# A graph kernel's message stage in groups of 1024 edges instead of 640, with bfloat16 parts summed in PSUM

## The chip, the cores and the metric

The kernel runs on one core of one Trainium2 chip. The metric is device time in microseconds (us), and lower is better. A core has five engines with instruction queues of their own: TensorE (PE; its weight loads are listed as PEld), VectorE (DVE), ScalarE (ACT), GpSimd (POOL) and SyncE (SP). They wait for one another by semaphores. SBUF is the on-chip memory of 128 partitions, PSUM the accumulators that TensorE writes.

## What is computed

A graph of 12,500 nodes with 128 features has 400,000 edges, sorted by target node. Two graph layers run one after the other, each with a residual and a layer norm. The first layer sums neighbours twice; the change leaves it alone. The second layer makes one message for each edge and sums the messages by target:

```python
ef  = relu(edge_attr @ We1 + be1) @ We2 + be2        # 64 -> 128 -> 128, by edge
ef  = ef * sigmoid(ts @ Wt + bt)                     # ts: edge_weight
msg = relu(concatenate([x[row], ef], axis=1) @ Wn1 + bn1) @ Wn2 + bn2
out = segment_sum(msg, col, num_segments=12500) + x
x   = layernorm(x + out)
```

Targets are drawn as 12500 times the square of a uniform number, so that the first nodes have many edges each and the last ones few.

## The kernel before

The program has three stages. Two of them sum neighbours (`sum_neighbours`, tiles named `sum_x_` and `sum_z_`), and the third makes and sums the messages (`sum_messages`, tiles named `messages_`). A tile is 128 edges, one to a partition; there are 3125. The second stage has already written, for each node, `y_d` = its features times the upper half of Wn1, plus the bias, and `rest_d`, what is left of the output beside the message sum.

The third stage goes by groups of 5 tiles (640 edges), 625 in all. In slot `s` of a fully unrolled program every engine has its share of several groups at different lags:

- GpSimd gathers the rows of `y_d` for the source nodes, one indirect DMA a tile (L1630), into a ring of 10 groups (`DEPTH`). It starts group g once the window sums of group g-10 are done (`sums_ready`).
- TensorE (in this order in a slot): `p_hid` of group s from the edge attributes (L1673, float32), `p_msg` of group s-3 (L1679), `p_edge` of group s-1 (L1686), and the window sums of group s-5 (L1696): the message rows times a one-hot matrix of 64 columns, in float32. A float32 product stands in the trace as two matmuls.
- ScalarE: relu to `hid` (L1711), sigmoid to `gate` (L1715), relu of the message rows in place (L1719).
- VectorE: adds a 64-node window to the node sums (L1750), adds `p_msg` to the gathered rows (L1755), makes `gated` = (`p_edge` + bias) times `gate` (L1760), and builds the one-hot matrix (L970).
- SyncE loads attributes and edge weights by bodies of 5 groups, the weights copied to all 128 partitions (L1641, L1644).

Whenever 256 nodes have their sums complete, a piece (`third_nodes`, 49 of them) multiplies them with Wn2, adds `rest_d`, takes the layer norm and stores. The order is written out by hand, by the lags `MSG_LAG, WIN_LAG, ADD_LAG = 3, 5, 6`.

## Time and profile before

| what | us |
|---|---|
| time, median of 3 runs | 9389.36 |
| the 3 runs | 9377.11 to 9419.71 |
| the profiled execution, span from first to last instruction | 9374.2 |
| of it the third stage, from its first gather (4711.19) to the end | 4663 |

The profiled execution's own time is its span; it lies 15 us below the median of the runs. PE is busy for 71% of the span, POOL for 61%, DVE for 46% and ACT for 23%. Busy time of POOL is the making of gathers; issuing a DMA is not counted. "idle <-X" after a row is the time in which the engine did nothing before that instruction, and who released it; "issue" means that the profile shows no wait, and "remote" that it shows a semaphore update with no instruction of this core just before it.

### The profile page before, as it was taken

The page shows a single profiled execution, that of the slowest core. Times are in us where ns is not written, and L with a number is a line of the kernel's source. Part 1 is how long each engine was busy: PE and PEld are TensorE (multiplying, and loading weights), DVE is VectorE, ACT ScalarE, POOL GpSimd, SP SyncE. Part 2 cuts the span into 40 slices and gives each one's busy share as a digit, 9 for nine tenths or more (in the row PEclk, how much of TensorE's full clock was granted, in tenths as well). Part 3 has the DMA queues.
Part 4 walks back from the last instruction along what each step waited for, and adds up shares of the span by engine and source line. Part 5 has one row for each costly group of instructions (what it writes and reads, how often), then busy time and mean ns, then how long its engine had stood idle before and what let it go on. Part 6 is the DMA issues. An engine that isn't in the chain of part 4 may idle for free.

```text
span 9374.2 us, 116910 instructions
## 1 busy us (share of the span) xinstructions
PE 6689.7 (71%) x36831; PEld 4954.1 (53%) x36831; DVE 4268.2 (46%) x9331; ACT 2188.8 (23%) x3195; POOL 5712.6 (61%) x5857
## 2 busy tenths in 40 slices
PE   4667777777656777767657777777777777777777
PEld 3455454444434555555545565565555555555555
DVE  6878777766634444444223233333333333333333
ACT  2111111111110000000023333333333333333333
POOL 6666555555546655655556666666666666666665
PEclk8788888888868888888767777777777777878777
DMA  3456666666647777777533333333333333333333
GB/s 101 128 174 204 200 225 227 221 223 217 223 136 254 243 252 250 257 245 252 192 121 118 109 112 117 109 117 113 110 118 114 110 112 123 112 114 121 113 118 93
DMA packets 585993, 1522.62 MB, mean 162 GB/s; under 512 B 148847, under 2 KB 362243, under 8 KB 558244
## 3 DMA queue, kind: packets, MB, share of 16 engines
q1 hardware_dynamic: 398177, 1131.24, 34.9%
q0 software_dynamic: 187200, 383.76, 14.7%
q8 instruction: 314, 5.14, 0.2%
q14 instruction: 302, 2.47, 0.1%
HBM read 1373.03 MB, written 141.47 MB: 162 GB/s over the span
## 4 chain that ended last, share of the span: by engine, by line
another core or an unknown queue 20%; PE 16%; issue 7%; DVE 4%; ACT 2%; DVEq 1%; DMA 0%; SPq 0%; ACTq 0%
PE messages_p_msg L1679 5%; PE messages_p_edge L1686 5%; PE messages_win L1696 4%; PE messages_p_hid L1673 3%; DVE messages_rows L1755 2%; ACT messages_hid L1711 1%; DVE messages_gated L1760 1%; ACT messages_gate L1715 1%; DVE messages_hot L970 1%; DVEq L62 0%; DVEq L1747 0%; DVE messages_sums L1750 0%; PE messages_win L1538 0%; ACT messages_rows L1719 0%
## 5 line engine op out<-in xcount | busy, mean ns | idle before, releaser
L1630 POOL DMA_INDIRECT messages_rows<-y_d,src_idx x3125 | 2992.2, 957 | 1694.2 <-issue 875.3
L1104 POOL DMA_INDIRECT sum_x_rows<-in_x,sum_x_edges x1525 | 1556.4, 1021 | 1084.4 <-PE sum_x_win L1194 514.6
L1104 POOL DMA_INDIRECT sum_z_rows<-z_d,sum_z_edges x1200 | 1162.6, 969 | 846.0 <-issue 322.4
L1679 PE MATMUL messages_p_msg<-Wm_e,messages_gated 128*128 128x128 f32 x6250 | 1127.9, 343 | 706.4 <-DVE messages_rows L1755 365.8
L1679 PEld LDWEIGHTS messages_p_msg<-Wm_e,messages_gated 128*128 128x128 f32 x6250 | 989.6, 244 | 1037.0 <-issue 996.4
L1755 DVE TENSOR_TENSOR messages_rows<-messages_p_msg,messages_rows 128x640 f32<-128x640 f32 x625 | 513.4, 821 | 1697.2 <-remote 1151.0
L1686 PE MATMUL messages_p_edge<-messages_hid,We 128*128 128x320 f32 x2500 | 1014.7, 539 | 254.7 <-DVE messages_gated L1760 128.3
L1206 PE MATMUL sum_x_build<-sum_x_key_hot,sum_x_low_hot 128*128 128x490 bf16 (+2 forms) x2900 | 869.6, 387 | 338.0 <-DVE sum_x_counts L1402 247.0
L1696 PEld LDWEIGHTS messages_win<-messages_hot,messages_rows 128*128 128x128 f32 x6250 | 947.0, 220 | 237.2 <-issue 164.9
L1696 PE MATMUL messages_win<-messages_hot,messages_rows 128*128 128x64 f32 x6250 | 909.1, 296 | 93.5 <-issue 67.5
L1711 ACT ACTIVATE messages_hid<-messages_p_hid,be 128x640 f32<-128x640 f32 x625 | 495.2, 792 | 1954.4 <-remote 1574.5
L1226 PE MATMUL sum_z_p_loaded<-sum_z_split,sum_z_counts 128*128 128x384 bf16 x2744 | 832.7, 364 | 141.7 <-DMA sum_z_split<-z_parts_d 110.9
L1402 DVE SCALAR_TENSOR_TENSOR sum_x_counts<-sum_x_counts,sum_x_build 128x980 f32 (+3 forms) x635 | 647.7, 1020 | 454.9 <-PE sum_x_build L1206 327.3
L1760 DVE SCALAR_TENSOR_TENSOR messages_gated<-messages_p_edge,be,messages_gate 128x640 f32<-128x640 f32 x625 | 550.6, 881 | 662.8 <-remote 434.1
L1226 PE MATMUL sum_x_p_prod<-sum_x_split,sum_x_counts 128*128 128x385 bf16 x2744 | 705.4, 351 | 180.8 <-DMA sum_x_split<-x_parts_d 144.5
L1686 PEld LDWEIGHTS messages_p_edge<-messages_hid,We 128*128 128x128 f32 x2500 | 543.1, 241 | 443.4 <-issue 317.7
L1190 PEld LDWEIGHTS sum_x_win<-sum_x_hot,sum_x_rows 128*128 128x128 f32 x3050 | 628.6, 223 | 228.7 <-issue 93.1
L1719 ACT ACTIVATE messages_rows<-messages_rows 128x640 f32<-128x640 f32 x625 | 457.8, 733 | 1103.7 <-DVE messages_rows L1755 636.2
L1673 PE MATMUL messages_p_hid<-messages_attr,We 64*128 64x320 f32 x2500 | 581.9, 545 | 185.6 <-ACT messages_hid L1711 157.1
L1402 DVE SCALAR_TENSOR_TENSOR sum_z_counts<-sum_z_counts,sum_z_build 128x784 f32 x325 | 336.6, 1036 | 804.9 <-DMA bm<-in_L_gnn_bn 409.9
L1297 ACT CAST sum_x_hot<-sum_x_hot 128x320 bf16<-128x320 f32 x305 | 139.7, 458 | 2111.8 <-DVE sum_x_hot L970 1436.9
L1190 PE MATMUL sum_x_win<-sum_x_hot,sum_x_rows 128*128 128x64 f32 x3050 | 569.7, 277 | 81.6 <-ACT sum_x_hot L1297 50.6
(250 smaller groups left out, 7916.5 us busy)
## 6 DMA issues: line engine op xcount, KB each, us to landing
sum_x_split<-x_parts_d SPq DMA_DIRECT2D x392, 675.5 KB
sum_z_split<-z_parts_d SPq DMA_DIRECT2D x392, 675.5 KB
messages_when<-in_edge_weight SPq DMA_DIRECT2D x125, 1600.0 KB
messages_attr<-in_edge_attr SPq DMA_DIRECT2D x125, 800.0 KB
counts_d<-sum_x_counts SPq DMA_DIRECT2D x28, 3136.0 KB
sum_z_counts<-counts_d SPq DMA_DIRECT2D x56, 1568.0 KB
messages_rows<-y_d,src_idx POOLq DMA_INDIRECT x3125
sum_x_rows<-in_x,sum_x_edges POOLq DMA_INDIRECT x1525
```

Of the source, the lines that this page charges most:

```text
L1104: nc.gpsimd.indirect_dma_start(out=rows[:, s % depth, j, :], out_offset=None, in_=table, in_offset=bass.IndirectOffsetOnAxis(ap=edges[:, b ...
L1190: last = nc.tensor.matmul(win[g % 2][:, 0:WIN], rows[:, g % depth, j, :], hot[:, q, j, :], start=j == 0, stop=j == TILES - 1)
L1206: last = nc.tensor.matmul(build[i % builds][:, h, 0:columns], low_hot[:, u % lows, :], hot_rooms(u)[:, h * columns:(h + 1) * columns], sta ...
L1226: last = nc.tensor.matmul(product_of(b)[0][:, 0:columns], by_count(b)[:, hi, :], split[:, n % XCHUNKS, hi % CHUNK, 0:columns], start=hi == ...
L1402: nc.vector.scalar_tensor_tensor(nodes, nodes, CARRY_MAX, summed_counts, ALU.min, ALU.add).then_inc(copied, 1)
L1630: nc.gpsimd.indirect_dma_start(out=rows[:, g % DEPTH, j, :], out_offset=None, in_=d["y"], in_offset=bass.IndirectOffsetOnAxis(ap=t.src_idx ...
L1673: last = nc.tensor.matmul(p_hid[:, h, 0:HALF], t.We1[own, :], attr[own, body % LOADS, g % UNROLL, :], start=True, stop=True)
L1679: last = nc.tensor.matmul(msg[:, j * P:(j + 1) * P], gated[:, g % GATEDS, j * P:(j + 1) * P], t.Wm_e[:], start=True, stop=True)
L1686: last = nc.tensor.matmul(p_edge[:, h, 0:HALF], t.We2[:], hid[:, g % HIDS, h, :], start=True, stop=True)
L1696: last = nc.tensor.matmul(win[g % 2][:, 0:WIN], rows[:, g % DEPTH, j, :], hot[:, g % WINDOW_HOTS, j, :], start=j == 0, stop=j == TILES - 1)
L1755: nc.vector.tensor_tensor(at, msg[:, 0:GROUP], at, ALU.add).then_inc(msg_added, 1)
L1760: nc.vector.scalar_tensor_tensor(gated[:, g % GATEDS, :].rearrange("p (h c) -> p h c", h=2), p_edge[:, :, 0:HALF], t.be2[:, 0:1], gate[:, ...
```

## The change

The third stage goes by groups of 8 tiles (1024 edges), 391 of them, and sums nodes in another way.

- The 3125 gathers stay as they are. The ring is 7 groups of 8 tiles, and a group is started when the last part of the group 7 before it has been made (`low_ready`), and no longer when its window sums are done.
- The relu'd message rows are split into three bfloat16 parts that add up to them: ScalarE writes the high part, VectorE subtracts it from the relu (`rest`), ScalarE rounds the rest to the middle part, VectorE subtracts once more for the low part. That is one instruction more on ScalarE and two more on VectorE in each group, for one fewer window addition on VectorE.
- The one-hot matrix has 128 columns in bfloat16. It is now the weights, and the three parts together (384 columns) stream through it. The sums stay in PSUM over a block, a run of tiles whose nodes should span at most 113: 114 blocks in all, the first of 297 tiles, the last ones of 14. At a block's end ScalarE copies the three sums (384 columns), TensorE turns them by three products with the identity (`flip_block`), and VectorE adds them to the node sums.
- The lags are 2 for `p_msg` and 5 for the window sums. These stand second in TensorE's slot. A block's turn stands first in the next slot, and a piece's product now stands ahead of `p_edge`.
- `hid` has 2 buffers for 3, `gate` 3 for 4, `gated` 2 for 3. SyncE loads by groups of 8 tiles, 3 groups ahead.
- Once, in slots 8 to 13, VectorE does some 60 small instructions that find out whether the plan fits the data, on top of the conversion of the target numbers that it did before.

TensorE in the middle of the stage, one slot before:

```order
L1673 MATMUL messages_p_hid<-messages_attr,We 128x320 x2
L1679 MATMUL messages_p_msg<-Wm_e,messages_gated 128x128 x5
L1686 MATMUL messages_p_edge<-messages_hid,We 128x320 x2
L1696 MATMUL messages_win<-messages_hot,messages_rows 128x64 x5
L1673 MATMUL messages_p_hid<-messages_attr,We 128x320 x2
```

and after, two slots, in the first of which a block has ended:

```order
L1738 MATMUL messages_win<-identity,messages_product 128x128 x3
L1771 MATMUL messages_p_hid<-messages_attr,We 128x512 x2
L1756 MATMUL messages_win<-messages_parts,messages_hot 128x384 x8
L1779 MATMUL messages_p_msg<-Wm_e,messages_gated 128x128 x8
L1791 MATMUL messages_p_edge<-messages_hid,We 128x512 x2
L1771 MATMUL messages_p_hid<-messages_attr,We 128x512 x2
L1756 MATMUL messages_win<-messages_parts,messages_hot 128x384 x8
L1779 MATMUL messages_p_msg<-Wm_e,messages_gated 128x128 x8
L1791 MATMUL messages_p_edge<-messages_hid,We 128x512 x2
L1738 MATMUL messages_win<-identity,messages_product 128x128 x3
```

The window sums went from the end of the slot to its start, the turn of a block stands ahead of everything, and a group has 4 + 8 + 16 + 4 = 32 matmuls of the trace for 8 tiles where it had 4 + 10 + 4 + 10 = 28 for 5.

VectorE in the middle of the stage, one slot before (names: `messages_hot` is the one-hot matrix, `messages_rows` the gathered rows):

```order
L970 TENSOR_TENSOR messages_hot<-iota,rel 128x320
L1747 TENSOR_LOAD base_int
L1747 ISA x2
L1750 ISA
L1750 TENSOR_TENSOR messages_sums<-messages_sums,messages_win 128x64
L1755 TENSOR_TENSOR messages_rows<-messages_p_msg,messages_rows 128x640
L1760 SCALAR_TENSOR_TENSOR messages_gated<-messages_p_edge,be,messages_gate 128x640
```

and after, a slot that begins with a block's addition (`messages_parts` are the bfloat16 parts):

```order
L1864 TENSOR_LOAD messages_bases
L1864 ISA x2
L1867 ISA
L1867 TENSOR_TENSOR messages_sums<-messages_sums,messages_win 128x128
L1884 TENSOR_TENSOR messages_parts<-messages_rows,messages_parts 128x8x128
L1887 SCALAR_TENSOR_TENSOR messages_rows<-messages_rows,messages_parts 128x1024
L1893 TENSOR_TENSOR messages_rows<-messages_p_msg,messages_rows 128x1024
L1898 SCALAR_TENSOR_TENSOR messages_gated<-messages_p_edge,be,messages_gate 128x1024
L1903 TENSOR_TENSOR messages_hot<-iota,rel 128x1024
L1884 TENSOR_TENSOR messages_parts<-messages_rows,messages_parts 128x8x128
```

Three instructions now read two tiles of SBUF each (`parts`, `rows`, `hot`), and they stand one behind another around the end of a slot; before there was one, the one-hot, of 320 elements.

The core of the diff:

```diff
+SPAN, BLOCK_NODES = 8, 113
+SPAN_DEPTH, SPAN_PARTS, SPAN_HOTS = 7, 3, 3
+SPAN_LOADS, SPAN_AHEAD = 4, 3
+SPAN_HIDS, SPAN_GATES, SPAN_GATEDS = 2, 3, 2
+SPAN_MSG_LAG, SPAN_WIN_LAG = 2, 5
+SPAN_SPACING, SPAN_SOON, SPAN_CHECK = 3, 16, 12
...
-                wait_for(pool, sums_ready, g - DEPTH + 1)
+            for g in range(plan.groups):
+                if g in (0, SPAN_SOON):
+                    pool.wait_ge(keep_in[1 if g else 0], 48)
+                wait_for(pool, low_ready, g - SPAN_DEPTH + 1)
                 pool.sem_inc(gathers_started, 1)
-                for j in range(TILES):
+                for j in range(tiles_of(g)):
+                    at = g * SPAN + j
                     nc.gpsimd.indirect_dma_start(
-                        out=rows[:, g % DEPTH, j, :], out_offset=None, in_=d["y"],
-                        in_offset=bass.IndirectOffsetOnAxis(ap=t.src_idx[:, g, j:j + 1], axis=0)).then_inc(rows_arrived[g % DEPTH], 16)
-            for q in range(DEPTH):
-                pool.wait_ge(rows_arrived[q], len(range(q, m.NG, DEPTH)) * 16 * TILES)
+                        out=rows[:, g % SPAN_DEPTH, j, :], out_offset=None, in_=d["y"],
+                        in_offset=bass.IndirectOffsetOnAxis(ap=src_idx[:, at:at + 1], axis=0)).then_inc(rows_arrived[g % SPAN_DEPTH], 16)
...
+            def load_group(g):
+                own = g % SPAN_LOADS
+                wait_for(sp, hid_summed, g - SPAN_LOADS + 1)
+                sp.dma_start(attr[:, own], d["span_attr"][g]).then_inc(attr_arrived[own], 16)
+                wait_for(sp, gate_ready, g - SPAN_LOADS + 1)
+                sp.dma_start(when[:, own], d["edge_weight"][g * SPAN * P:(g + 1) * SPAN * P].partition_broadcast(P)
                              ).then_inc(when_arrived[own], 16)
...
+            def flip_block(b):
+                pe.wait_ge(block_copied, b + 1)
+                for i in range(SPLITS):
+                    last = nc.tensor.matmul(win[b % 2][:, 0:P], product[:, b % 2, i * P:(i + 1) * P], t.identity[:],
+                                            start=i == 0, stop=i == SPLITS - 1)
+                last.then_inc(block_flipped, 1)
+
+            def open_block(b, s):
+                wait_for(pe, block_added, b - 1)
...
+            def window_sums(g, s):
+                pe.wait_ge(low_ready, g + 1)
+                pe.wait_ge(hot_ready, g + 1)
+                for j in range(tiles_of(g)):
+                    b = plan.block_of[g * SPAN + j]
+                    begin, end = plan.blocks[b]
+                    if g * SPAN + j == begin:
+                        open_block(b, s)
+                    last = nc.tensor.matmul(win[b % 2][:, 0:SPLITS * P], hot[:, g % SPAN_HOTS, j, :], parts[:, g % SPAN_PARTS, j, :],
+                                            start=g * SPAN + j == begin, stop=g * SPAN + j == end - 1)
+                last.then_inc(win_summed, 1)
...
+                for b in ended_at[s - 1] if s else []:
+                    flip_block(b)
...
+                for g in groups(s, SPAN_WIN_LAG):
+                    window_sums(g, s)
+                for g in groups(s, SPAN_MSG_LAG):
                     pe.wait_ge(gated_ready, g + 1)
                     wait_for(pe, msg_added, g)
-                    for j in range(TILES):
-                        last = nc.tensor.matmul(msg[:, j * P:(j + 1) * P], gated[:, g % GATEDS, j * P:(j + 1) * P], t.Wm_e[:],
+                    for j in range(tiles_of(g)):
+                        last = nc.tensor.matmul(p_msg[:, j * P:(j + 1) * P], gated[:, g % SPAN_GATEDS, j * P:(j + 1) * P], t.Wm_e[:],
                                                 start=True, stop=True)
                     last.then_inc(msg_summed, 1)
...
+                for g in groups(s, SPAN_MSG_LAG + 1):
+                    act.wait_ge(rest_ready, g + 1)
+                    nc.scalar.copy(part(g, 1), room(g)).then_inc(middle_ready, 1)
...
-                    nc.scalar.activation(rows[:, g % DEPTH], rows[:, g % DEPTH], ACT.Relu).then_inc(msg_ready, 1)
+                    wait_for(act, win_summed, g - SPAN_PARTS + 1)
+                    nc.scalar.activation(part(g, 0), room(g), ACT.Relu).then_inc(high_ready, 1)
...
+                for b in ended_at[s]:
+                    act.wait_ge(win_summed, s - SPAN_WIN_LAG + 1)
+                    wait_for(act, block_flipped, b - 1)
+                    nc.scalar.copy(product[:, b % 2], win[b % 2][:, 0:SPLITS * P]).then_inc(block_copied, 1)
...
+                nc.vector.tensor_copy(tile_bases[:, own], tile_bases[:, own].bitcast(I32)).then_inc(rel_ready, 1)
+                dve.wait_ge(rel_ready, 4 * i + 2)
+                nc.vector.tensor_tensor(rel[:, own], rel[:, own], tile_bases[:, own], ALU.subtract).then_inc(rel_ready, 1)
+                dve.wait_ge(rel_ready, 4 * i + 3)
+                nc.vector.memset(tile_bases[:, own], 0.0).then_inc(rel_ready, 1)
...
+            def add_block(b):
+                nodes = ds(dve.value_load(bases[0:1, b:b + 1], min_val=0, max_val=m.N), P)
+                dve.wait_ge(block_flipped, b + 1)
+                wait_for(dve, block_added, b)
+                nc.vector.tensor_tensor(sums[:, nodes], sums[:, nodes], win[b % 2][:, 0:P], ALU.add).then_inc(block_added, 1)
...
+                for g in groups(s, SPAN_MSG_LAG + 2):
+                    dve.wait_ge(middle_ready, g + 1)
+                    nc.vector.tensor_tensor(part(g, 2), room(g), part(g, 1), ALU.subtract).then_inc(low_ready, 1)
+                for g in groups(s, SPAN_MSG_LAG + 1):
+                    dve.wait_ge(high_ready, g + 1)
+                    nc.vector.scalar_tensor_tensor(room(g), room(g), 0.0, part(g, 0), ALU.max, ALU.subtract).then_inc(rest_ready, 1)
+                for g in groups(s, SPAN_MSG_LAG):
+                    before = sum(16 * tiles_of(i) for i in range(g % SPAN_DEPTH, g + 1, SPAN_DEPTH))
+                    dve.wait_ge(rows_arrived[g % SPAN_DEPTH], before)
                     dve.wait_ge(msg_summed, g + 1)
-                    at = rows[:, g % DEPTH].rearrange("p j f -> p (j f)")
-                    nc.vector.tensor_tensor(at, msg[:, 0:GROUP], at, ALU.add).then_inc(msg_added, 1)
+                    at = room(g).rearrange("p j f -> p (j f)")
+                    nc.vector.tensor_tensor(at, p_msg[:, edges_of(g)], at, ALU.add).then_inc(msg_added, 1)
                 for g in groups(s, 1):
                     dve.wait_ge(gate_ready, g + 1)
                     dve.wait_ge(edge_summed, g + 1)
-                    wait_for(dve, msg_summed, g - GATEDS + 1)
-                    nc.vector.scalar_tensor_tensor(gated[:, g % GATEDS, :].rearrange("p (h c) -> p h c", h=2),
-                                                   p_edge[:, :, 0:HALF], t.be2[:, 0:1],
-                                                   gate[:, g % GATES], ALU.add, ALU.mult).then_inc(gated_ready, 1)
-                for g in groups(s, MSG_LAG):
-                    wait_for(dve, sums_ready, g - WINDOW_HOTS + 1)
-                    one_hot(nc, t, hot[:, g % WINDOW_HOTS], t.rel[:, g, :]).then_inc(hot_ready, 1)
+                    wait_for(dve, msg_summed, g - SPAN_GATEDS + 1)
+                    nc.vector.scalar_tensor_tensor(gated[:, g % SPAN_GATEDS, :], p_edge[:], t.be2[:, 0:1],
+                                                   gate[:, g % SPAN_GATES], ALU.add, ALU.mult).then_inc(gated_ready, 1)
+                for g in groups(s, SPAN_WIN_LAG - 1):
+                    n = tiles_of(g)
+                    wait_for(dve, win_summed, g - SPAN_HOTS + 1)
+                    nc.vector.tensor_tensor(
+                        hot[:, g % SPAN_HOTS, 0:n], t.iota[:].unsqueeze(1).to_broadcast([P, n, P]),
+                        rel[:, g * SPAN:g * SPAN + n].unsqueeze(2).to_broadcast([P, n, P]), ALU.is_equal).then_inc(hot_ready, 1)
```

## Rows read from the trace of the kernel before

**Rows 1.** The page: span, then busy time of each engine.
```profile
span 9374.2 us, 116910 instructions
...
PE 6689.7 (71%) x36831; PEld 4954.1 (53%) x36831; DVE 4268.2 (46%) x9331; ACT 2188.8 (23%) x3195; POOL 5712.6 (61%) x5857
```

**Rows 2.** Windows: us; busy (instructions) PE, PEld, DVE, ACT, POOL; PEclk; DMA; GB/s.
```profile
6000.00:7000.00 1000.00, 742.97 (x3834) 582.80 (x3834) 317.74 (x607) 337.52 (x439) 645.51 (x676) 0.78 0.36 113
```

**Rows 3.** Groups by line, 4711-9374 us: busy us, mean ns, idle before, releasers.
```profile
L1630 POOL DMA_INDIRECT messages_rows<-y_d,src_idx x3125 | 2992.2, 957 | 1694.2 <-issue 875.3 <-remote 490.9 <-PE messages_win L1696 268.1
L1679 PE MATMUL messages_p_msg<-Wm_e,messages_gated 128*128 128x128 f32 x6250 | 1127.9, 343 | 706.4 <-DVE messages_rows L1755 365.8 <-issue 340.0
L1686 PE MATMUL messages_p_edge<-messages_hid,We 128*128 128x320 f32 x2500 | 1014.7, 539 | 254.7 <-DVE messages_gated L1760 128.3 <-issue 74.1 <-ACT messages_hid L1711 51.9
...
L1696 PE MATMUL messages_win<-messages_hot,messages_rows 128*128 128x64 f32 x6250 | 909.1, 296 | 93.5 <-issue 67.5 <-DVE messages_piece_u L1546 25.2
L1673 PE MATMUL messages_p_hid<-messages_attr,We 64*128 64x320 f32 x2500 | 581.9, 545 | 185.6 <-ACT messages_hid L1711 157.1 <-issue 14.5 <-DMA messages_attr<-in_edge_attr 13.3
...
L1755 DVE TENSOR_TENSOR messages_rows<-messages_p_msg,messages_rows 128x640 f32<-128x640 f32 x625 | 513.4, 821 | 1697.2 <-remote 1151.0 <-PE messages_p_msg L1679 315.6 <-issue 230.3
...
L970 DVE TENSOR_TENSOR messages_hot<-iota,rel 128x320 f32<-128x320 f32 x625 | 303.6, 486 | 0.0
```

**Rows 4.** Timeline, a steady stretch: start us, us, engine, line, idle before.
```profile
6503.57 0.94 POOL L1630 DMA_INDIRECT messages_rows<-y_d,src_idx  x1 [2.76 <-PE messages_win L1696]
...
6504.53 2.50 PE L1679 MATMUL messages_p_msg<-Wm_e,messages_gated 128*128 128x128 f32 x10
...
6507.14 0.82 DVE L1755 TENSOR_TENSOR messages_rows<-messages_p_msg,messages_rows 128x640 f32<-128x640 f32 x1 [1.91 <-PE messages_p_msg L1679]
...
6510.34 1.38 PE L1679 MATMUL messages_p_msg<-Wm_e,messages_gated 128*128 128x128 f32 x10
...
6517.11 0.82 DVE L1755 TENSOR_TENSOR messages_rows<-messages_p_msg,messages_rows 128x640 f32<-128x640 f32 x1 [7.00 <-remote]
...
6525.61 0.94 POOL L1630 DMA_INDIRECT messages_rows<-y_d,src_idx  x1 [3.44 <-remote]
```

**Rows 5.** Timeline, same stretch: one-hot instruction and two gathers.
```profile
6504.62 0.48 DVE L970 TENSOR_TENSOR messages_hot<-iota,rel 128x320 f32<-128x320 f32 x1
...
6504.81 1.11 POOL L1630 DMA_INDIRECT messages_rows<-y_d,src_idx  x1 [0.30 <-issue]
...
6506.23 0.94 POOL L1630 DMA_INDIRECT messages_rows<-y_d,src_idx  x1 [0.30 <-issue]
```

**Rows 6.** Timeline, first stage: VectorE instructions and gathers under them.
```profile
128.01 1.08 DVE L1406 TENSOR_TENSOR sum_x_counts<-sum_x_counts,sum_x_split 128x896 f32<-128x896 f32 x1
128.04 1.87 POOL L1104 DMA_INDIRECT sum_x_rows<-in_x,sum_x_edges  x1 [0.30 <-issue]
...
1000.92 0.82 DVE L1382 TENSOR_TENSOR sum_x_low_hot<-iota,sum_x_low_part 128x640 bf16<-128x640 f32 x1
1001.28 1.35 POOL L1104 DMA_INDIRECT sum_x_rows<-in_x,sum_x_edges  x1 [1.78 <-remote]
...
1002.42 1.17 DVE L1402 SCALAR_TENSOR_TENSOR sum_x_counts<-sum_x_counts,sum_x_build 128x980 f32 x1
1002.93 0.94 POOL L1104 DMA_INDIRECT sum_x_rows<-in_x,sum_x_edges  x1 [0.30 <-issue]
```

**Rows 7.** Timeline: POOL near the start and end of the stage.
```profile
4711.19 0.94 POOL L1630 DMA_INDIRECT messages_rows<-y_d,src_idx  x1 [59.55 <-DMA rel<-in_dst_tiles]
...
4786.30 0.95 POOL L1630 DMA_INDIRECT messages_rows<-y_d,src_idx  x1 [12.77 <-PE messages_win L1696]
...
9337.04 0.95 POOL L1630 DMA_INDIRECT messages_rows<-y_d,src_idx  x1 [0.30 <-issue]
```

**Rows 8.** Groups by line, 0-4700 us: forms like the added ones.
```profile
L1226 PE MATMUL sum_z_p_loaded<-sum_z_split,sum_z_counts 128*128 128x384 bf16 x2744 | 832.7, 364 | 141.7 <-DMA sum_z_split<-z_parts_d 110.9 <-issue 19.4 <-DVE sum_z_sums L1331 5.7
...
L1235 PE MATMUL sum_z_p_loaded<-identity,sum_z_loaded_product 128*128 128x128 f32 x168 | 37.3, 380 | 24.1 <-ACT sum_z_loaded_product L1314 21.1 <-issue 3.1
```

## Prediction before the run

> **What bounds the kernel now.** I read the page first, for the whole span [rows 1]; then the windows of the third stage [rows 2] and its groups by line [rows 3], for who is busy and who waits; then a steady stretch of the timeline [rows 4], to see which wait ends last.
>
> The third stage's gathers run from 4711.19 to 9337.99 us [rows 7], 4626.8 us for 3125 gathers, 1.48 us each. POOL's busy time is 2992.2 us (957 ns each) and its idle time 1694.2 us, of which 59.55 us stand before the first gather [rows 3, 7]. About 0.30 us between two gathers is issue [rows 5], in all 3124 x 0.30 = 937 us. So a gather that nobody disturbs costs 0.945 + 0.30 = 1.25 us, and 1694.2 - 59.55 - 937 = 697 us are real waits. Without waits or disturbance the gathers would need 3125 x 1.25 = 3906 us: the floor of this stage. It is a floor that the change can't lower, since it keeps all gathers.
>
> Why does POOL wait? TensorE's four groups of matmuls are busy 1127.9 + 1014.7 + 909.1 + 581.9 = 3633.6 us [rows 3], which is 5.81 us in each of the 625 slots, while a slot lasts 4626.8 / 625 = 7.40 us. The 1.6 us between is what TensorE loses by waiting (and by the pieces). The timeline shows one way in which it is lost [rows 4]. TensorE's `p_msg` ends at 6504.53 + 2.50 = 6507.03, and the row addition of VectorE starts 0.11 us later. The next `p_msg` ends at 6510.34 + 1.38 = 6511.72, but VectorE, which has been idle for 7.00 us, starts its addition only at 6517.11, 5.4 us late. Between the two POOL had begun a train of gathers, and the late one is released by "remote". I read this so: after some microseconds of unbroken gathers, TensorE's completions reach the others late. The row addition's idle time is 1697.2 us in the stage, 1151.0 us of it "remote" [rows 3]. So the loop is TensorE, late signal, VectorE, TensorE; once the ring is full, POOL waits for the loop too, mostly 2.8 to 3.4 us at a time [rows 4]. Neither engine alone is the bound: POOL's floor is 3906 us, TensorE's busy time 3634 us.
>
> **The change: TensorE.** Hidden layer, edge and message products keep their work for a tile: (581.9 + 1014.7 + 1127.9) / 3125 = 0.872 us. The window sum of a tile goes from 909.1 / 3125 = 0.291 us to one bfloat16 product of 384 columns. The second stage has that shape: 832.7 / 2744 = 0.303 us [rows 8]. New are 114 turns of 3 products, each two matmuls in the trace: 684 x 37.3 / 168 = 152 us, 0.049 us for a tile [rows 8]. Sum 1.224 us, 9.79 us for a group of 8. Together 3825 us, 190 us more than now; it is hidden where TensorE waits anyway, and its price is bounded by 0 and 190 us. What the change saves is slots: 391 for 625, so 234 times fewer crossings from TensorE to another engine and back. If a slot goes on losing 1.6 us, TensorE's loop lasts 9.79 + 1.63 = 11.42 us, 391 of them 4465 us, against 4627 us now. The granted clock is 0.78 in the middle of the stage [rows 2], and I leave it there: fewer matmuls stand for a tile (4.0 instead of 5.6), but they are longer.
>
> **VectorE.** Three instructions now have two inputs in SBUF and 1024 elements: `low`, `rest` and the one-hot. The nearest rows are 0.82 us for 640 and 1.08 us for 896 elements [rows 6], which continued gives about 1.21 us for 1024. The row addition becomes 0.821 + 384 x 0.001 = 1.2 us, `gated` about the same. That is some 6.2 us in a slot of 11.4 us, so VectorE is no bound by itself; DVE is busy 318 us in 1000 now [rows 2].
>
> Their effect on GpSimd is a cost, though. A gather that begins under such an instruction ends only after it. The one-hot of 0.48 us makes a gather 1.11 us, the next gather has 0.94 us [rows 5]. The one of 0.82 us makes it 1.35 us, that of 1.08 us makes it 1.87 us; and a VectorE instruction of 1.17 us that reads one of its inputs from PSUM leaves it at 0.94 us [rows 6]. If instructions fall at random in a train with a gather each 1.25 us, one of length d holds a gather with probability d / 1.25, for d / 2 on average: d x d / 2.5. For 0.486 us this gives 0.094 us; the trace has 3125 x (957 - 945) ns = 37.5 us over 625 one-hots, 0.06 us each [rows 3], 64% of it. For 1.21 us the formula gives 0.586 us, 64% of it is 0.375 us. The group has three of them close together, which makes it likelier that a gather meets one, so I take 0.45 us, between the two. There are 3 x 391 = 1173: **528 us**. The ends are 0.1 us each (117 us, if gathers slip between them as they mostly do with the one-hot now) and 0.586 us each (687 us). The one-hots' present 37 us are in the 528, since I count from the undisturbed gather.
>
> The Trainium skill has a rule for this ("SBUF — State Buffer", section "Who interferes with whom"): a VectorE instruction with two SBUF inputs contends with a GpSimd instruction that reads SBUF, and whoever comes second blocks. By that rule, the trace agrees that the gather is held (1.87 for 0.94 us) and that one PSUM input avoids it. It speaks against this change, which moves work from TensorE's window product to exactly such instructions. In full it would make each of the 1173 hold POOL for its whole 1.21 us; that is the fourth case below.
>
> **ScalarE.** 338 us busy in 1000 now [rows 2], for three instructions of 640 elements in a slot. One more, and 1024 for 640 elements: (338 x 4 / 3) per edge, 45% busy. Hidden, at no cost unless the loop below takes it in. **SyncE** issues two loads a group, 782 where it had 250. TensorE waits 13.3 us in the stage for them now [rows 3]; cover is 3 groups, some 34 us. Nothing.
>
> **The ring.** 7 x 8 = 56 tiles for 50, and a place is free at `low`, 4 slots after the slot number of its group, where it was 5 slots. In time that is 4 x 11.6 = 46 us for 5 x 7.4 = 37 us. The first ring of gathers is followed now by a wait of 12.77 us [rows 7], which stays about as it is.
>
> **Ends.** After the last gather come 36 us now (9374.2 - 9337.99). The last slots are longer and hold one step more: +20 us (bounds 0 and 40). The 60 small checks of VectorE in slots 8 to 13 lie under the full ring of gathers.
>
> **Sum.** Gathers 3906 + holds 528 = 4434 us; TensorE's loop is at 4465 us, so the two meet, and I add 100 us of waits (bounds 0 and the present 697): 4534 us. Against 4627 us that is -93. With the end +20: -73. The profiled execution, 9374.2 us, becomes 9301 us; the median of the runs lies 15 us above it: **9315 us**.
>
> **Rivals.**
> *B, TensorE's late completions keep the loop long (slower).* With POOL's trains unbroken, lateness may grow with the train instead of counting by slot. The row addition then waits in VectorE's queue with `gated` and the one-hot behind it, and TensorE waits for both. If a slot loses twice what it loses now, 3.26 us, it lasts 13.05 us, 391 of them 5103 us: +476, with the end +20 and the 15: 9885 us. It decides from the point where TensorE's idle time in a slot is over 1.8 us (then the loop passes 4534). For it: 1151.0 us of "remote" [rows 3]. Against it: an unbroken train is what makes them late, and B itself breaks the trains.
> *C, the holds stay small and the waits go.* 3906 + 117 + 100 = 4123 us: -504, so 9374.2 - 504 + 20 + 15 = 8905 us. For it: TensorE at full pace would do it, and the trace has 0.06 us a hold now. Against it: TensorE's loop would have to lose little in a slot, 4123 / 391 - 9.79 = 0.75 us.
> *D, each two-input instruction holds POOL in full.* 1173 x 1.21 = 1419 us: 3906 + 1419 + 100 = 5425 us, +798, 10,207 us. The trace speaks against it, since a hold ends with the instruction (1.35 us for 0.82).
> *E, the plan doesn't fit the data.* Then the stage is made a second time in the general way, 14,000 us or more. Blocks are cut at 113 expected nodes for 128 columns, so I give it next to nothing.
>
> **Chances.** The forecast 0.38; its own range is 9180 to 9440 us, since a hold of 0.375 or 0.586 us instead of 0.45 moves it by -88 or +159 us, and waits of 50 instead of 100 us by -50; B (9440 to 9990) 0.30; C (8800 to 9180) 0.27; D and E 0.05. The range leaves out the fast third of C and a tail of B with D: 8880 to 9870. A measurement of this kernel can tell about 0.5% from no change, 9342 to 9436 us. Faster: C and two thirds of the forecast's case, 0.52. Within: 0.11. Slower: the rest, 0.37.
>
> **What would show it.** The mean of one gather in the profile after: 945 + 1173 x 0.45 / 3125, about 1.11 us, in my case; 0.98 in C; 1.4 in D. POOL's idle time in the stage beyond the first and 0.30 us a gather: about 100 us in my case, 600 in B. The granted clock near 0.78; `win` near 0.30 us a product; `low`, `rest` and the one-hot near 1.2 us. I am wrong if these instructions are much shorter or longer, if the window product costs over 0.4 us, or if something that no row shows (bfloat16 writes, ScalarE's four instructions) becomes the end of the chain.

## The result, and the profile after

The changed kernel takes 9569.73 us (median of 4 runs, 9541.55 to 9598.91), the kernel before beside it 9386.33 us. The ratio is **1.0191**, with a 95% interval of 1.017 to 1.0212: 1.9% slower. I had forecast 9315 us and 0.8% faster. The time lies outside my own range (9180 to 9440 us) and in that of my rival B (9440 to 9990 us), 3% under its price of 9885 us.

Span and busy time of each engine, from the page of the changed kernel (before: [rows 1]):

```profile
span 9539.4 us, 104096 instructions
...
PE 6088.1 (64%) x32520; PEld 3959.4 (42%) x32520; DVE 5222.8 (55%) x8964; ACT 2481.2 (26%) x2996; POOL 6116.3 (64%) x5857
```

TensorE has 600 us less to do than before, VectorE 950 us more, and the whole is 165 us longer. The groups by line of the third stage, changed kernel; they answer to [rows 3] (busy us, mean ns | idle before, releasers):

```profile
L1699 POOL DMA_INDIRECT messages_rows<-y_d,src_idx x3125 | 3388.0, 1084 | 1436.0 <-issue 950.8 <-DVE messages_parts L1884 424.4 <-DMA messages_sums<-in_message_base 60.8
...
L1779 PE MATMUL messages_p_msg<-Wm_e,messages_gated 128*128 128x128 f32 x6250 | 875.0, 300 | 49.0 <-DVE messages_gated L1898 49.0
L1791 PE MATMUL messages_p_edge<-messages_hid,We 128*128 128x512 f32 x1564 | 740.9, 595 | 6.3 <-issue 6.3
L1756 PE MATMUL messages_win<-messages_parts,messages_hot 128*128 128x384 bf16 x3125 | 731.4, 388 | 1450.6 <-DVE messages_hot L1903 1150.9 <-issue 296.7 <-DVE messages_piece_u L1552 2.8
...
L1893 DVE TENSOR_TENSOR messages_rows<-messages_p_msg,messages_rows 128x1024 f32<-128x1024 f32 x391 | 478.4, 1224 | 1930.3 <-remote 1223.1 <-PE messages_p_msg L1779 349.2 <-DMA messages_rows<-y_d,src_idx 213.6
...
L1771 PE MATMUL messages_p_hid<-messages_attr,We 64*128 64x512 f32 x1564 | 479.5, 692 | 48.0 <-issue 18.4 <-ACT messages_hid L1802 16.2 <-DMA messages_attr<-in_span_attr 13.3
...
L1884 DVE TENSOR_TENSOR messages_parts<-messages_rows,messages_parts 128x1024 bf16<-128x1024 f32 x391 | 475.9, 1217 | 0.0
...
L1738 PE MATMUL messages_win<-identity,messages_product 128*128 128x128 f32 x684 | 126.2, 330 | 465.7 <-ACT messages_product L1822 323.3 <-issue 142.5
```

The last gather, which answers to [rows 7]:

```profile
9472.43 0.95 POOL L1699 DMA_INDIRECT messages_rows<-y_d,src_idx  x1 [0.31 <-issue]
```

From these rows the books of GpSimd can be made as in the prediction. From the first to the last gather it is 9473.4 - 4710.2 = 4763 us (4627 before). The undisturbed gathers are 3906 us as ever. What the gathers take above 0.945 us is 3388.0 - 2953 = 435 us (39 before; I forecast 528). The rest, 4763 - 3906 - 435 = 422 us, are waits (682 before by the same sum; I forecast 100). So +396 of holds and -260 of waits make +136 us, and the tail behind the last gather grew from 36 to 66 us (I forecast 56). The prediction had 697 us for the waits before, because it took 0.30 us between two gathers; the median gap is 0.305 us in both traces, and only with that do the 3906 us come out.

Those books tell where GpSimd's time went, not why it waited 422 us. TensorE's five groups are busy 875.0 + 740.9 + 731.4 + 479.5 + 126.2 = 2953 us, 7.6 us of a slot of 4763 / 391 = 12.2 us. It loses 4.6 us a slot, where it lost 1.6. Not all of that is a loss that a better order could win back. The gathers of a slot with their holds take (3906 + 435) / 391 = 11.1 us, and TensorE can't be faster than that: 3.5 of the 4.6 us are GpSimd's pace, and in 1.1 us GpSimd waits too. Before the change the two were 0.5 and 1.1 us.

Two rows name the waits: 1450.6 us before the window sums, 1150.9 of them for the one-hot (before the change all idle time before them was 93.5 us), and 1930.3 us of VectorE before the row addition, 1223.1 of them "remote".

The timeline has two states. This is the good one, from the middle of the stage (start us, us, engine, line, idle before):

```profile
6306.33 1.97 POOL L1699 DMA_INDIRECT messages_rows<-y_d,src_idx  x1 [0.30 <-issue]
...
6308.44 1.88 PE L1791 MATMUL messages_p_edge<-messages_hid,We 128*128 128x512 f32 x4
...
6308.71 1.23 DVE L1893 TENSOR_TENSOR messages_rows<-messages_p_msg,messages_rows 128x1024 f32<-128x1024 f32 x1 [1.23 <-PE messages_p_msg L1779]
...
6310.41 1.28 DVE L1898 SCALAR_TENSOR_TENSOR messages_gated<-messages_p_edge,be,messages_gate 128x1024 f32<-128x1024 f32 x1 [0.48 <-PE messages_p_edge L1791]
...
6311.61 1.21 DVE L1903 TENSOR_TENSOR messages_hot<-iota,rel 128x1024 bf16<-128x1024 f32 x1
...
6312.97 1.46 PE L1756 MATMUL messages_win<-messages_parts,messages_hot 128*128 128x384 bf16 x8 [1.59 <-DVE messages_hot L1903]
...
6313.95 1.97 POOL L1699 DMA_INDIRECT messages_rows<-y_d,src_idx  x1 [0.30 <-issue]
...
6314.27 1.95 PE L1779 MATMUL messages_p_msg<-Wm_e,messages_gated 128*128 128x128 f32 x16
...
6316.32 1.23 DVE L1893 TENSOR_TENSOR messages_rows<-messages_p_msg,messages_rows 128x1024 f32<-128x1024 f32 x1 [1.23 <-PE messages_p_msg L1779]
```

A slot lasts 6316.32 - 6308.71 = 7.61 us, for 8 tiles. It is a closed chain: `p_edge` ends at 6310.32, then `gated`, then the one-hot to 6312.82, and only then TensorE's window sums, for which it has been idle 1.59 us, then `p_msg` and `p_edge`. In each slot one gather lasts 1.97 us, begun under `rest`, and one 1.3 us, begun under the one-hot; the others take 0.94 us. GpSimd makes 5 gathers in such a slot where 8 tiles are used up, so the rows run out: counted from the gathers and row additions of the trace, 40 tiles were ready beyond the one in use at 6261 us, and 3 at 6378 us. This state can't last, but it isn't an empty ring that ends it here: no row addition between the two times waits for rows. Then comes the bad state:

```profile
6383.97 1.95 PE L1779 MATMUL messages_p_msg<-Wm_e,messages_gated 128*128 128x128 f32 x16
...
6396.12 1.23 DVE L1893 TENSOR_TENSOR messages_rows<-messages_p_msg,messages_rows 128x1024 f32<-128x1024 f32 x1 [10.99 <-remote]
...
6404.52 1.28 DVE L1898 SCALAR_TENSOR_TENSOR messages_gated<-messages_p_edge,be,messages_gate 128x1024 f32<-128x1024 f32 x1 [7.17 <-remote]
...
6407.08 2.72 PE L1756 MATMUL messages_win<-messages_parts,messages_hot 128*128 128x384 bf16 x8 [18.39 <-DVE messages_hot L1903]
...
6409.59 2.51 PE L1779 MATMUL messages_p_msg<-Wm_e,messages_gated 128*128 128x128 f32 x16
...
6417.62 2.08 PE L1771 MATMUL messages_p_hid<-messages_attr,We 64*128 64x512 f32 x4 [3.80 <-issue]
...
6443.74 0.94 POOL L1699 DMA_INDIRECT messages_rows<-y_d,src_idx  x1 [0.30 <-issue]
6452.19 1.23 DVE L1893 TENSOR_TENSOR messages_rows<-messages_p_msg,messages_rows 128x1024 f32<-128x1024 f32 x1 [42.22 <-remote]
...
6455.88 2.72 PE L1756 MATMUL messages_win<-messages_parts,messages_hot 128*128 128x384 bf16 x8 [36.19 <-DVE messages_hot L1903]
...
6457.68 1.15 POOL L1699 DMA_INDIRECT messages_rows<-y_d,src_idx  x1 [13.00 <-DVE messages_parts L1884]
```

`p_msg` ends at 6385.92 and its row addition starts at 6396.12, 10 us late, though the gathers of its group were made by 6383.39. The next ends at 6412.10, and its addition starts at 6452.19, **40 us late**, with VectorE idle for 42.22 us and TensorE, which needs the one-hot queued behind that addition, for 36.19 us. In these 40 us GpSimd makes gather upon gather of 0.95 us with nothing to hold it, until at 6444.68 its ring is full; it stands still, and 7.5 us later the addition starts, with `gated` ready right behind it. The trace also has records of many semaphore updates themselves. TensorE's update for this addition is recorded at 6452.10, 40 us behind the product, and that of the window sums, whose last product ended at 6409.80, at 6438.03. Over the stage, the recorded updates of VectorE and ScalarE stand 0.01 us behind the instruction's end (the median), and about 1% are over 1 us behind. Of those behind `p_msg`, 34% are over 1 us late (67% in the kernel before). What tips the good state into the bad one is not shown: the episode before this one began with 18 tiles ready, this one with 3. The windows of the two states and of the stage's middle (which answers to [rows 2]):

```profile
6284.00:6352.00 68.00, 54.10 (x280) 32.85 (x279) 48.67 (x43) 37.01 (x35) 54.28 (x46) 0.95 0.46 137
6396.00:6452.00 56.00, 8.82 (x32) 4.79 (x32) 6.53 (x9) 4.24 (x4) 37.10 (x39) 0.56 0.22 60
6000.00:7000.00 1000.00, 553.12 (x2690) 330.46 (x2690) 487.75 (x474) 376.00 (x367) 713.76 (x658) 0.81 0.38 109
```

The granted clock is 0.95 in the good state and 0.56 in the bad one, where TensorE is busy for 8.82 of 56 us: it falls after TensorE has stood idle (18.39 us, then 36.19 us), and it is a consequence here.

### The profile page after: what moved, and what is told of

It is laid out like the page before. It is cut to its first block, busy times and chain, and to the rows that moved or that the text cites. A ratio compares the mean times of both kernels' runs of the same rounds, so it can differ in the third digit from the quotient of the medians.

```text
span 9539.4 us, 104096 instructions
## 1 busy us (share of the span) xinstructions
PE 6088.1 (64%) x32520; PEld 3959.4 (42%) x32520; DVE 5222.8 (55%) x8964; ACT 2481.2 (26%) x2996; POOL 6116.3 (64%) x5857
## 4 chain that ended last, share of the span: by engine, by line
another core or an unknown queue 14%; PE 13%; DVE 10%; issue 6%; POOL 6%; ACT 1%; DVEq 0%; DMA 0%; SPq 0%; POOLq 0%; ACTq 0%
POOL messages_rows L1699 6%; PE messages_p_msg L1779 5%; PE messages_win L1756 4%; PE messages_p_edge L1791 3%; DVE messages_hot L1903 3%; DVE messages_gated L1898 2%; DVE messages_rows L1893 2%; DVE messages_rows L1887 1%; DVE messages_parts L1884 1%; PE messages_p_hid L1771 1%; PE messages_win L1738 1%; DVEq L68 0%; ACT messages_product L1822 0%; DVE messages_sums L1867 0%
## 5 line engine op out<-in xcount | busy, mean ns | idle before, releaser
L1699 POOL DMA_INDIRECT messages_rows<-y_d,src_idx x3125 | 3388.0, 1084 | 1436.0 <-issue 950.8
L1756 PE MATMUL messages_win<-messages_parts,messages_hot 128*128 128x384 bf16 x3125 | 731.4, 388 | 1450.6 <-DVE messages_hot L1903 1150.9
L1893 DVE TENSOR_TENSOR messages_rows<-messages_p_msg,messages_rows 128x1024 f32<-128x1024 f32 x391 | 478.4, 1224 | 1930.3 <-remote 1223.1
L1756 PEld LDWEIGHTS messages_win<-messages_parts,messages_hot 128*128 128x128 bf16 x3125 | 316.8, 110 | 2017.4 <-issue 1897.1
L1779 PE MATMUL messages_p_msg<-Wm_e,messages_gated 128*128 128x128 f32 x6250 | 875.0, 300 | 49.0 <-DVE messages_gated L1898 49.0
L1814 ACT ACTIVATE messages_parts<-messages_rows 128x1024 bf16<-128x1024 f32 x391 | 412.2, 1054 | 1433.2 <-DVE messages_rows L1893 954.6
L1791 PE MATMUL messages_p_edge<-messages_hid,We 128*128 128x512 f32 x1564 | 740.9, 595 | 6.3 <-issue 6.3
L1898 DVE SCALAR_TENSOR_TENSOR messages_gated<-messages_p_edge,be,messages_gate 128x1024 f32<-128x1024 f32 x391 | 501.2, 1282 | 329.1 <-remote 197.8
L1802 ACT ACTIVATE messages_hid<-messages_p_hid,be 128x1024 f32<-128x1024 f32 x391 | 434.3, 1111 | 734.1 <-remote 394.0
L1394 DVE TENSOR_SCALAR sum_x_key_hot<-columns,sum_x_key 128x980 bf16<-128x980 f16 (+3 forms) x1600 | 608.3, 422 | 25.7 <-remote 19.3
L1805 ACT CAST messages_parts<-messages_rows 128x1024 bf16<-128x1024 f32 x391 | 407.9, 1043 | 766.9 <-DVE messages_rows L1887 553.8
```

The lines of the kernel that those rows point to most:

```text
L1394: nc.vector.tensor_scalar(hot_rooms(u), t.columns[:, 0:columns], key[:, ring, at:at + 1], None, ALU.is_equal).then_inc(key_hot_ready, 1)
L1699: nc.gpsimd.indirect_dma_start(out=rows[:, g % SPAN_DEPTH, j, :], out_offset=None, in_=d["y"], in_offset=bass.IndirectOffsetOnAxis(ap=src_ ...
L1756: last = nc.tensor.matmul(win[b % 2][:, 0:SPLITS * P], hot[:, g % SPAN_HOTS, j, :], parts[:, g % SPAN_PARTS, j, :], start=g * SPAN + j == ...
L1779: last = nc.tensor.matmul(p_msg[:, j * P:(j + 1) * P], gated[:, g % SPAN_GATEDS, j * P:(j + 1) * P], t.Wm_e[:], start=True, stop=True)
L1791: last = nc.tensor.matmul(p_edge[:, own], t.We2[:], hid[:, g % SPAN_HIDS, own], start=True, stop=True)
L1893: nc.vector.tensor_tensor(at, p_msg[:, edges_of(g)], at, ALU.add).then_inc(msg_added, 1)
```

## The experiments

Theory L: while GpSimd makes gathers without a break, TensorE's completions reach the others late, the more the longer the train; a break in the train lets them in. (I call a break a pause or a standstill below; GpSimd may be busy in it, but makes no gather.) Theory H is the one of my prediction: two-input instructions of VectorE hold gathers and are a pure cost. Theory C: the change made the loop longer by its order, above all the one-hot behind `gated`. "Slot" is below the mean time between two row additions, from all of them in a trace. All ratios are to the kernel before on the same chip; the chips differ by 1.4% (medians of before from 9384 to 9512 us), so spans are compared by ratio. The slots are not scaled, and no difference of them under 1.4% is read. "Held" is what the gathers take above 0.945 us each; the last column sums the releasers other than issue and the load before the first gather (waits ahead of a pause too), and holds the 0.30 us of issue of each wait.

| kernel | ratio, 95% interval | slot, us | held, us | waits for the ring, us |
|---|---|---|---|---|
| before | 1 | 7.41 (5 tiles) | 39 | 759 |
| changed | 1.0191 (1.017 to 1.0212) | 12.27 | 435 | 424 |
| a_depth4 | 1.0251 (1.0223 to 1.0279) | 12.53 | 426 | 567 |
| a_reduce2 | 1.0699 (1.067 to 1.0728) | 13.58 | 100 | 1277 |
| a_reduce2_pause | 1.0126 (1.0091 to 1.016) | 12.07 | 153 | 0, and 759 of pauses |
| a_hotfirst | 1.0091 (1.0067 to 1.0116) | 12.12 | 579 | 250 |
| a_hotflip | 1.0047 (1.0033 to 1.0061) | 11.89 | 613 | 136 |
| a_hotflip_pause | 1.0253 (1.0222 to 1.0285) | 12.50 | 562 | 2, and 475 of pauses |
| a_hotflip_two | 1.0403 (1.037 to 1.0435) | 12.93 | 166 | 962 |
| b_hold | 1.000 (0.9984 to 1.0017) | 7.51 | 246 | 596 |
| b_pause | 0.997 (0.9955 to 0.9985) | 7.48 | 34 | 517, and 339 of pauses |
| b_pause_mid | 0.9941 (0.9924 to 0.9958) | 7.34 | 39 | 187, and 572 of pauses |
| b_pause_long | 0.9912 (0.9882 to 0.9943) | 7.33 | 15 | 17, and 759 of pauses |
| b_pause_eight | 1.0018 (1.0002 to 1.0033) | 7.43 | 26 | 336, and 474 of pauses |

**The loop without gathers.** The third stage gathers its first ring and goes on with stale rows: `for g in range(plan.groups)` on GpSimd becomes `for g in range(SPAN_DEPTH)` (`DEPTH` in the kernel before), and VectorE waits for the first ring alone.

> The changed kernel, but the third stage gathers only its first ring (56 tiles) and then goes on adding to the stale rows; all other instructions stay. Theory L (late signals: TensorE's completions reach VectorE and ScalarE late while GpSimd gathers without a break, the more the longer the train): every slot is as short as the short ones of the full kernel, 7.6 us, so the stage lasts 391 x 7.6 + 60 = 3030 us and the span is about 7,750 us. Rival S (TensorE's loop is slow by itself, whatever GpSimd does): slots stay at 12.2 us on average, and the span stays within 2% of 9540 us.

> The kernel before, with gathers for the first ring (50 tiles) alone, the rest of the stage on stale rows. Theory L: slots of about 4.4 us, 625 x 4.4 + 60 = 2810 us, span about 7,520 us, so that the loop of before is, for a tile, a little faster than that of the change. Rival S: slots stay at 7.4 us, span about 9,370 us.

Measured: spans of 8060.8 and 7511.3 us, 0.848 and 0.790 of before. TensorE in the kernel before, and in the changed one, from 5000 to 6000 us:

```profile
5000.00:6000.00 1000.00, 1000.00 (x6690) 804.53 (x6689) 546.72 (x1014) 580.64 (x746) 0.00 (x0) 1.00 0.33 119
```

```profile
5000.00:6000.00 1000.00, 796.60 (x4259) 471.16 (x4256) 778.06 (x703) 583.16 (x553) 0.00 (x0) 1.00 0.33 104
```

Rival S is gone: without gathers the slots are 4.31 us before and 8.28 us after the change. Late completions are gone as well: in the kernel before without gathers, under 1% of the recorded updates behind `p_msg` are over 1 us late. But for the changed kernel I had expected 7.6, and this is the first finding on the change itself. Before, TensorE is busy all of the time at full clock. In the changed kernel it is busy 80%: its loop is no longer its own work but the chain through VectorE. For the whole stage the loop alone is 391 x 8.28 = 3237 us against 625 x 4.31 = 2694 us, **543 us more**, although TensorE has less to do. With gathers this is no loss of 543 us, since GpSimd's floor of 3906 us stands above both loops. What it can take away is the room to catch up after a late completion.

**Is it GpSimd, or the traffic?** In one kernel every second tile is gathered after the first ring; in the other SyncE loads all rows, the same number of bytes to the same places, in plain transfers:

```diff
-                for j in range(tiles_of(g)):
+                for j in range(0, tiles_of(g), 1 if g < SPAN_DEPTH else 2):
```

```diff
+            def load_rows(g):
+                wait_for(sp, low_ready, g - SPAN_DEPTH + 1)
+                for j in range(tiles_of(g)):
+                    first = (g * SPAN + j) * 37 % (m.N // P) * P
+                    sp.dma_start(rows[:, g % SPAN_DEPTH, j, :], d["y"][first:first + P]).then_inc(rows_arrived[g % SPAN_DEPTH], 16)
```

> The changed kernel with only every second tile gathered after the first ring (1,594 gathers for 3,125; the other tiles use stale rows). By the runs, the first ring alone gives 8,061 us and all gathers 9,540 us. Theory N (each gather costs TensorE's loop the same, 0.48 us): 8,061 + 1,538 x 0.48 = 8,800 us. Theory L (what costs is unbroken trains; a half-loaded GpSimd waits for its ring most of the time): under 8,450 us.

> The changed kernel with all rows of the third stage loaded by SyncE in plain transfers of 128 x 512 bytes (the rows are then others than the graph's; GpSimd makes one gather for a spare tile and no more): the same bytes into the same places, no indirect transfers. Theory G (what makes TensorE's completions late is GpSimd making gathers): as without gathers, about 8,061 us, delays over 5 us nearly none. Rival D (it is the traffic of the rows on the transfer engines and in SBUF): delays stay, and the span is over 9,200 us.

Measured: 8010 and 7951 us in all, 0.853 and 0.847 of before on their chip, as without any gathers (0.848). The windows of the two:

```profile
5000.00:6000.00 1000.00, 797.11 (x4250) 471.17 (x4248) 775.38 (x707) 583.89 (x556) 522.96 (x517) 1.00 0.45 138
```

```profile
5000.00:6000.00 1000.00, 798.03 (x4258) 472.23 (x4256) 775.74 (x711) 585.66 (x558) 0.00 (x0) 1.00 0.54 171
```

With 171 GB/s moved for 109 in the full kernel nothing is late (no "remote" before the row addition, 1223.1 us in the full kernel), so it is not the traffic. And 517 gathers in 1000 us, in trains of four, cost TensorE nothing: slots of 8.27 us, 57.1 us of "remote". A price of 0.48 us for each gather is refuted. The full kernel's slot is 4 us longer, with 658 gathers in 1000 us in trains of 50 on average, but that compares unlike things: GpSimd alone needs 11.1 us for a slot's gathers there. What is left for the late completions is the making of gathers on GpSimd. That it takes an unbroken train, the pauses below show, with all gathers made.

**The ring.** `SPAN_DEPTH` 7 to 4.

> The changed kernel with a ring of 4 groups (32 tiles) for 7, nothing else. Theory L: GpSimd reaches the end of its ring sooner, so that each late episode is cut short after some 20 gathers: the longest delay of a row addition behind its product falls from 40 us to under 20, trains get shorter, and the time is 9,250 to 9,540 us in spite of the smaller ring. Rival R (the ring is what covers GpSimd's waits): GpSimd's waits grow from 420 us, the time is over 9,650 us.

1.0251 against 1.0191 of the changed kernel. The longest delay of a row addition behind its product fell from 56 to 25 us (I had read 40 and expected under 20), but those over 5 us went from 68 to 94, and GpSimd waits 567 us. The time I expected under L, 9,250 to 9,540 us, was too low (1.0251 of 9386 us is 9622 us): cutting episodes short paid less than the smaller ring cost.

**Without two thirds of the holds.** `rest` and `low` become one-input reductions of the same length (1209 and 1208 ns for 1217 and 1216), and what they should have made is left out:

```diff
-                    nc.vector.tensor_tensor(part(g, 2), room(g), part(g, 1), ALU.subtract).then_inc(low_ready, 1)
+                    nc.vector.tensor_reduce(taken[:, g % 4, 0:tiles_of(g)], room(g), axis=AX.X, op=ALU.max).then_inc(low_ready, 1)
```

> The changed kernel with rest and low (two SBUF inputs each) replaced by reductions of the same 1024 elements with one input; what they should have made is left out, so the middle and low parts are wrong. Only the one-hot still has two SBUF inputs. Theory H (the holds are what the change costs): what gathers take above 0.945 us falls from 435 us to about 145 us, and the time falls by as much, to about 9,280 us. Theory L (the time is set by late signals): the holds fall alike, but GpSimd's unbroken trains make TensorE late as often or more, GpSimd waits more instead, and the time stays within 1% of 9,570 us or rises.

```profile
L1700 POOL DMA_INDIRECT messages_rows<-y_d,src_idx x3125 | 3053.4, 977 | 2296.2 <-DVE messages_taken L1887 1276.6 <-issue 954.1 <-DMA messages_sums<-in_message_base 65.5
...
L1896 DVE TENSOR_TENSOR messages_rows<-messages_p_msg,messages_rows 128x1024 f32<-128x1024 f32 x391 | 478.4, 1224 | 2443.1 <-remote 1922.6 <-PE messages_p_msg L1780 341.6 <-issue 178.9
```

The holds fell as theory H said, from 435 to 3053.4 - 2953 = 100 us. And the kernel became 5% **slower**. "Remote" before the row addition rose from 1223.1 to 1922.6 us, GpSimd's waits from 424.4 to 1276.6 us. Nothing in VectorE's times differs; its instructions just no longer stop GpSimd, as the timeline shows for a gather under a reduction:

```profile
6614.27 1.21 DVE L1890 TENSOR_REDUCE messages_taken<-messages_rows 128x8 f32<-128x1024 f32 x1
6614.35 0.94 POOL L1700 DMA_INDIRECT messages_rows<-y_d,src_idx  x1 [0.31 <-issue]
```

So the holds had kept a part of TensorE's completions on time: a part, since 1223.1 us of "remote" stand in the changed kernel with them.

**A standstill instead of the holds.** The same kernel, and GpSimd clears a tile nobody reads (1320 elements on a partition) after each 5 gathers:

```diff
+                    if at and at % 5 == 0:
+                        wait_for(pool, paused, at // 5 - 1)
+                        nc.gpsimd.memset(still[:], 0.0).then_inc(paused, 1)
```

> The kernel in which rest and low are one-input reductions (their results left out; 1.070 of before), and GpSimd clears a tile of 1320 elements (by the 0.54 us of 512 elements about 1.4 us) after each 5 gathers: 624 pauses as long as a held gather, 870 us in all. Theory P (the relief that two-input instructions give TensorE is that GpSimd stands still for over a microsecond): late row additions get much rarer (sum of delays over 1 us from 1,720 us to under 900) and the time falls to 0.99 to 1.04 of before, in spite of the pauses. Rival Q (the relief has to do with VectorE's second port or with when the holds fall, not with the standstill): delays stay, and the time stays at 1.07 or rises.

```profile
L1704 POOL DMA_INDIRECT messages_rows<-y_d,src_idx x3121 | 3101.9, 994 | 863.9 <-issue 863.9
...
L1703 POOL MEMSET messages_still<- 128x1320 f32 x624 | 759.2, 1217 | 0.2
...
L1900 DVE TENSOR_TENSOR messages_rows<-messages_p_msg,messages_rows 128x1024 f32<-128x1024 f32 x391 | 478.4, 1224 | 2189.4 <-DMA messages_rows<-y_d,src_idx 2056.5 <-PE messages_p_msg L1784 115.4 <-issue 17.5
```

Adding 759 us of work to the engine that was said to be the bound takes 5.4% off: 1.0126, less than the changed kernel. GpSimd waits for nobody, and the row addition's idle time has changed its releaser from "remote" to the arrival of rows. The pauses last 1.22 us, not the 1.4 I assumed. One sign that I had named did not come: the delays over 1 us sum to 1203 us, not under 900. But the additions now wait for rows; none is "remote" any more, and of the recorded updates behind `p_msg` 5% are over 1 us late (60% in a_reduce2). Theory P holds: the relief is the break in the gathers, whoever brings it about.

**The chains of the change.** The one-hot moves from the end of VectorE's slot to its start (a_hotfirst), and in addition the block's turn from ahead of `p_hid` to behind it (a_hotflip), so that `p_hid` may cover ScalarE's copy.

```diff
+                for g in groups(s, SPAN_WIN_LAG - 1):
+                    n = tiles_of(g)
+                    wait_for(dve, win_summed, g - SPAN_HOTS + 1)
...
                 for g in groups(s, SPAN_MSG_LAG + 2):
                     dve.wait_ge(middle_ready, g + 1)
```

```diff
-                for b in ended_at[s - 1] if s else []:
-                    flip_block(b)
...
                     last.then_inc(hid_summed, 1)
+                for b in ended_at[s - 1] if s else []:
+                    flip_block(b)
                 for g in groups(s, SPAN_WIN_LAG):
                     window_sums(g, s)
```

> The changed kernel with one edit: VectorE makes the one-hot of a slot before the other instructions of the slot (ahead of low), not after gated. Theory C (the change has put the one-hot at the end of a closed chain: row addition, gated, one-hot, window sums, p_msg): TensorE no longer waits for it, the 1150.9 us of idle time before the window sums nearly go, and a late row addition no longer stops the window sums; 150 to 350 us less than the changed kernel, about 9,300 us (scaled to the chip of that profile). Theory L alone (only late signals and gathers count): the lost time moves to another wait, and the time stays within 0.7% of the changed kernel.

> The same edit in the kernel that gathers its first ring alone (stale rows after it). Theory C: slots fall from 8.28 us on average to about 7.0 us, the span from 8,061 us to about 7,560 us, since TensorE needs 6.4 us a slot at full clock. If VectorE or ScalarE is the next bound, they stay above 7.6 us and the span above 7,800 us.

> The changed kernel with the one-hot first in VectorE's slot (as in the run before) and a block's turn on TensorE behind p_hid, not ahead of it, so that ScalarE's copy of the block is covered by p_hid. Theory C (closed chains that the change made are a part of the loss): TensorE's wait for the copy (323 us before the turn's products in the changed kernel) goes, and 30 to 100 us of it are gained over the kernel with the one-hot first, which was at 1.009 of before: 0.998 to 1.006 of before. Theory L alone (only gathers and late signals): within 0.3% of 1.009.

> The kernel with the one-hot first and the turn behind p_hid, gathering its first ring alone (stale rows after it). Theory C (these two chains are what the change lengthened): the mean slot falls from 8.28 us in the changed kernel and 7.83 us with the one-hot first to about 7.2 us, the span from 7,914 to about 7,670 us. If the bound is VectorE's own work (some 6.9 us a slot with pieces), no less than 7.4 us and 7,740 us.

```profile
L1699 POOL DMA_INDIRECT messages_rows<-y_d,src_idx x3125 | 3532.2, 1130 | 1257.7 <-issue 947.2 <-DVE messages_parts L1890 250.4 <-DMA messages_sums<-in_message_base 60.0
...
L1756 PE MATMUL messages_win<-messages_parts,messages_hot 128*128 128x384 bf16 x3125 | 669.3, 358 | 239.1 <-issue 158.4 <-DVE messages_piece_u L1552 53.3 <-DVE messages_parts L1890 27.4
...
L1899 DVE TENSOR_TENSOR messages_rows<-messages_p_msg,messages_rows 128x1024 f32<-128x1024 f32 x391 | 477.8, 1222 | 1824.9 <-remote 951.3 <-DMA messages_rows<-y_d,src_idx 689.6 <-PE messages_p_msg L1779 145.7
```

```profile
L1699 POOL DMA_INDIRECT messages_rows<-y_d,src_idx x3125 | 3566.0, 1141 | 1156.1 <-issue 949.7 <-DVE messages_parts L1890 136.4 <-DMA messages_sums<-in_message_base 69.9
...
L1899 DVE TENSOR_TENSOR messages_rows<-messages_p_msg,messages_rows 128x1024 f32<-128x1024 f32 x391 | 478.0, 1223 | 1846.9 <-DMA messages_rows<-y_d,src_idx 1292.4 <-remote 475.3 <-issue 40.4
```

Alone, the loop falls from 8.28 to 7.83 and to 7.23 us a slot (I had expected 7.0 and 7.2 us); 391 x 7.23 = 2827 us still is 133 us more than before the change. With gathers, the time falls from 1.0191 to 1.0091 and to 1.0047 of before: 1.4 of the 1.9% lay in these two places. The gain of the first was below the 150 us that I expected, since the waits moved: the row addition now waits for rows (213.6, then 689.6, then 1292.4 us "<-DMA"), while "remote" falls from 1223.1 to 951.3 and 475.3 us. In a_hotflip GpSimd hardly waits (136.4 us), and gathers hold 613 us. It is the bound there: 3906 + 613 + 134 us of waits are all of its 4652 us from the first gather to the last, 25 us more than before the change. What the waits gave back (682 to 134 us), the holds took (39 to 613 us). One thing did not go as expected: the turn's products wait for ScalarE's copy for 428.2 us in a_hotflip and 398.6 us in a_hotfirst (323.3 in the changed kernel). That wait fell only in the loops without gathers, from 343.7 to 232.0 us. So the turn's new place helps, and not by hiding the copy as I had thought.

**Are the holds a cost now?** Two kernels from a_hotflip: a pause of 1.22 us after each 8 gathers; and two bfloat16 parts instead of three, so that `low`, a third of the two-input instructions, is left out, the sums are a little less exact, and TensorE streams 256 columns for 384. GpSimd is then released by `middle_ready`.

```diff
-                    nc.vector.tensor_tensor(part(g, 2), room(g), part(g, 1), ALU.subtract).then_inc(low_ready, 1)
...
-                    last = nc.tensor.matmul(win[b % 2][:, 0:SPLITS * P], hot[:, g % SPAN_HOTS, j, :], parts[:, g % SPAN_PARTS, j, :],
+                    last = nc.tensor.matmul(win[b % 2][:, 0:2 * P], hot[:, g % SPAN_HOTS, j, :], parts[:, g % SPAN_PARTS, j, 0:2 * P],
```

> The kernel with the one-hot first and the turn behind p_hid (1.005 of before), and GpSimd clears a tile of 1320 elements (about 1.4 us) after each 8 gathers, 390 pauses or 550 us. If late signals are still what costs, delays fall and the time falls to 0.98 to 1.00 of before. If GpSimd itself is the bound by now (it waits 134 us in the stage, and 613 us go into held gathers), the pauses come on top in good part: 1.02 to 1.05.

> The kernel with the one-hot first and the turn behind p_hid, and the message rows split into two bfloat16 parts, not three: low is left out, with 390 of the two-input instructions, and TensorE streams 256 columns for 384. GpSimd is started again when the middle part is made. If GpSimd and its holds are the bound by now: a third of the 613 us of holds goes, 0.975 to 0.99 of before. If the holds are needed as relief, delays grow instead and the time is 1.00 to 1.03.

```profile
L1699 POOL DMA_INDIRECT messages_rows<-y_d,src_idx x3125 | 3119.3, 998 | 1972.2 <-ACT messages_parts L1805 961.8 <-issue 945.4 <-DMA messages_sums<-in_message_base 64.9
...
L1896 DVE TENSOR_TENSOR messages_rows<-messages_p_msg,messages_rows 128x1024 f32<-128x1024 f32 x391 | 478.3, 1223 | 2228.1 <-remote 1986.6 <-PE messages_p_msg L1779 180.7 <-issue 60.4
```

The pauses end the late completions (9.2 us of "remote" before the row addition) and still cost: from the first gather to the last the stage takes 4885 us for 4652, since GpSimd is the bound. But taking holds away is worse still: the held time falls from 613 to 166 us, and the ratio is 1.0403, over the 1.00 to 1.03 that I expected, with 1986.6 us of "remote". Both neighbours of a_hotflip are slower. So the holds are not all waste there either: the `low` instructions take time of GpSimd, and without them the waits grow by more.

**The kernel before.** Two more one-hot matrices in each slot that nobody reads (b_hold), and pauses of 0.54, 1.22 and, by 960 elements, 0.92 us after each 5 gathers, and of 1.22 us after each 8.

```diff
+                    for i in range(2):
+                        nc.vector.tensor_tensor(extra[:, 2 * (g % 4) + i], t.iota[:].unsqueeze(1).to_broadcast([P, TILES, P]),
+                                                t.rel[:, g].unsqueeze(2).to_broadcast([P, TILES, P]), ALU.is_equal)
```

```diff
+                if g:
+                    wait_for(pool, paused, g - 1)
+                    nc.gpsimd.memset(still[:], 0.0).then_inc(paused, 1)
                 wait_for(pool, sums_ready, g - DEPTH + 1)
```

> The kernel before, and VectorE makes two one-hot matrices of 640 elements more in each slot, right after its own, which nobody reads: two more instructions of about 0.8 us with two SBUF inputs, 1,250 in all. Theory H (holds are a pure cost): each holds GpSimd by 0.17 to 0.26 us, so 210 to 330 us more, about 9,640 us on a chip with 9,386 us for the kernel before. Theory L with relief (a held gather gives TensorE's completions time to arrive): row additions that start over 1 us behind their product get rarer (188 before), and the time stays within 1% of before or falls.

> The kernel before, and GpSimd clears a small tile (512 elements on each partition, nobody reads it) once in each group of 5 gathers: a pause in the making of gathers of 0.4 to 1 us. Theory L with relief: TensorE's completions arrive promptly (sum of delays over 1 us from 1,982 us to under 1,000), GpSimd's waits for the ring nearly vanish, since the pauses take their place; time between -1% and +3% of before, by the length of the pause. Rival (it is not the making of gathers but GpSimd being busy at all that delays them): delays stay, waits stay, and the pauses come on top, 250 to 600 us.

> The kernel before with a pause of about 1.4 us (a tile of 1320 elements cleared) after each 5 gathers, where 0.54 us gave 0.997. GpSimd's floor becomes 3906 + 624 x 1.27 = 4,700 us for the stage, 70 us over its present 4,627. Theory P (a standstill over a microsecond is the relief): delays of row additions over 1 us fall from about 2,000 us to under 900, waits for the ring vanish, GpSimd alone is the bound: 1.005 to 1.015. Rival Q: delays stay as they are and the time is over 1.03.

> The kernel before with a pause by a tile of 960 elements, about 0.9 us, after each 5 gathers (0.54 us gave 0.997, 1.22 us gave 0.991 and no wait for the ring any more, so that GpSimd alone was the bound). GpSimd's floor is here some 3906 + 624 x 0.8 = 4,400 us, against 4,590 us used with the long pause. If a standstill of 0.9 us relieves enough: 0.975 to 0.99. If relief sets in only above it: waits for the ring come back to 200 us or more and the time is 0.99 to 1.00.

> The kernel before with the pause of 1.22 us after each 8 gathers, not 5: 390 pauses, GpSimd's floor some 3906 + 390 x 1.08 = 4,330 us. If what counts is the length of each pause: 0.97 to 0.99. If it is the number of gathers between two pauses (TensorE falls behind within a train of 8): waits for the ring come back, 0.99 to 1.01.

```profile
L1631 POOL DMA_INDIRECT messages_rows<-y_d,src_idx x3125 | 3199.6, 1024 | 1546.2 <-issue 888.3 <-remote 458.7 <-PE messages_win L1697 137.2
...
L1756 DVE TENSOR_TENSOR messages_rows<-messages_p_msg,messages_rows 128x640 f32<-128x640 f32 x625 | 513.5, 822 | 1426.1 <-remote 1228.4 <-PE messages_p_msg L1680 128.1 <-issue 68.0
```

```profile
L1634 POOL DMA_INDIRECT messages_rows<-y_d,src_idx x3125 | 2968.1, 950 | 921.5 <-issue 847.8 <-DMA rel<-in_dst_tiles 56.9 <-PE messages_win L1700 10.1
...
L1630 POOL MEMSET messages_still<- 128x1320 f32 x624 | 758.9, 1216 | 0.2
...
L1759 DVE TENSOR_TENSOR messages_rows<-messages_p_msg,messages_rows 128x640 f32<-128x640 f32 x625 | 515.4, 825 | 3015.7 <-DMA messages_rows<-y_d,src_idx 2973.2 <-PE messages_p_msg L1683 42.6
```

b_hold: 1,250 more two-input instructions add 207 us of held gathers and no time at all; GpSimd's waits pay for them (596 us for 759). Theory H, with 210 to 330 us, is refuted for this kernel too. The delays did not get rarer, though ("remote" 1228.4 for 1151.0 us; 168 row additions over 5 us behind their product for 167), so relief is not shown here: the holds only took the place of waits.

With pauses of 1.22 us, GpSimd hardly waits for the ring (17 us), "remote" is gone from the row addition, and the kernel is **0.9% faster than before** (interval 0.9882 to 0.9943), the fastest of those that gather all rows, though GpSimd does 759 us more. I had expected it 0.5 to 1.5% slower: I took 1.4 us for the pause, and a floor of 4,700 us where it uses 4,590. The shorter pauses give less (0.9941 with 187 us of waits left, 0.997 with 517), and trains of 8 with the long pause give nothing (1.0018). So both count, the length of the pause and the number of gathers between two.

Only the long pause after 5 ends the long delays: of the recorded updates behind `p_msg`, 30% are over 5 us late before and under 1% with it, 67% and 21% over 1 us. "Remote" before the row addition is 1372.7 us with 0.54 us, 1520.1 with 0.92 us and 1440.3 with trains of 8, more than the 1151.0 of before. I had expected the sum of the delays over 1 us, 1982 us before, to fall under 1,000 with the shortest pause; it is 2190 us. With the longest it is 2505 us, not under 900, but there the additions wait for rows. So the 0.6% of b_pause_mid didn't come from fewer late completions. Its longest delay is 14.2 us for 40.0; whether that is what pays, no run shows.

## Why the prediction was wrong, point by point

**The waits: the step that failed.** The sum was 3906 + 528 + 100 = 4534 us, measured were 3906 + 435 + 422 = 4763 us. So the term of 100 us, what GpSimd waits for TensorE's loop, was mis-sized by 322 us; the holds came out 93 us lower, the end 10 us higher. The 100 us stood on the sentence "If a slot goes on losing 1.6 us". That loss was read off as a constant of a slot, so that fewer slots would mean less loss. It was none: a slot of the changed kernel loses 4.6 us. Counted on GpSimd's side, the waits are 1.1 us a slot before and after, which looks like a constant after all. But with the same 391 slots they are 0.3 us in a_hotflip and 3.3 us in a_reduce2. Two things went in there. First, the order. I listed which instructions stand where, and did not follow the chain one slot round: `p_edge`, `gated`, one-hot, window sums, `p_msg`. In the kernel before, the one-hot is made two slots ahead of its use, so its place behind `gated` cost nothing; now it is one slot ahead, and the window sums stand second in TensorE's slot. That made the loop alone 543 us longer (3237 for 2694 us, with the turn's place in it), and undoing both gave 1.4% of the time with gathers. Second, the late completions. I saw the mechanism in [rows 4] and gave B its name, "lateness may grow with the train", but called an unbroken train B's own brake. The train is broken only when the ring is full, 40 us later.

**The holds: right in size, wrong in sign.** The rows gave 528 us, measured were 435 (0.37 us for each of 1173, at the lower value of my formula, 0.375). I booked them as a loss. In the changed kernel the absence of two thirds of them costs 5% (a_reduce2); in the kernel before, more of them cost nothing (b_hold). The reading of [rows 5, 6] was right, and what was missing is that an engine which is slowed may be the one whom another waits to be slowed. The rule of the Trainium skill ("SBUF — State Buffer", section "Who interferes with whom") describes the hold, and the trace agrees (a gather of 1.97 us under `rest`). The same section says that TensorE never waits on anyone there. By the runs, its completions came 10 and 40 us late in the stretch above, and 56 us at most in that trace, when GpSimd gathered unbroken; whether a port has to do with it no run here shows, and for the time the measurement decides.

**TensorE's work: mis-sized, and hidden.** I forecast 9.79 us a slot by adding shares of [rows 3]; it was 7.6 us, both under the 11.1 us of GpSimd's gathers and holds. For the same columns in longer products, `p_edge` took 740.9 us instead of 1014.7, `p_hid` 479.5 instead of 581.9; `p_msg`, whose form is the same, 875.0 instead of 1127.9.

**The tail**: +30 for +20 us. **The window product** (0.234 us a tile for 0.303), **SyncE's loads** (13.3 us of waiting as before) and **ScalarE** were no cost, as said.

**The case.** C (no waits, small holds) would have needed TensorE on time with GpSimd at full speed. No run shows both together; where holds were taken away, delays came. B was the case that came, at 0.30, and its mechanism is in the trace: the late row addition, with `gated` and the one-hot queued behind it. But its price of 9885 us was made by doubling a loss without a reason for the factor, on top of a busy time that was 2.2 us too long: 9.79 + 3.26 us a slot for 7.6 + 4.6. The two errors partly cancel, so that 9570 us lies in B's range is in part luck. My own range was too narrow even by its own terms: with holds of 0.586 us its upper end would have been 9474 us, not 9440, and it let the waits move by 50 us only, where their bounds were 0 and 697.

The loops alone don't split the loss into order and lateness. A slot is 3.1 us longer with gathers than without before the change, and 4.0 us after it, but GpSimd's pace is in both: its floor is 3906 us, the loops alone are 2694 and 3237 us. How much of the 422 and 682 us of waits is lateness, only runs that end the lateness tell, and they add pauses: the kernel before gains 0.9% net.

What stays open is why TensorE's completions are late: the rows show the products' records ending and the signals behind them late, and that it takes gathers made in an unbroken train. The profile models the ends of matmuls, so the rows can't tell a product that finishes late from a signal that travels late. The mechanism inside the chip is not shown.

## What to carry to other kernels

Follow the chain of a moved instruction once round its loop, with the lag of each step: a lag shortened by one slot can close a chain that was open. Run the loop with the suspected engine silent, before and after the change: it shows at once how long the order makes the loop. Then hold it against the pace of the suspected engine: a longer loop under that pace costs only its room to catch up. And before you book an engine's standstill as a loss, ask who gets on with his work in it.

## What the runs showed of the hardware

- TensorE's completions arrive late while GpSimd makes indirect gathers of 0.95 us every 1.25 us without a break: 10 us late, then 40 us, and 56 us at most in that stage. VectorE's and ScalarE's updates stay within 0.01 us (median). 517 gathers in 1000 us in trains of four leave them on time, and so do plain transfers of the same bytes.
- A pause of 1.22 us in the making of gathers after each 5 ends this, and makes two kernels faster, by 0.9% (before) and 5.4% (a_reduce2, 1.0699 to 1.0126). In the kernel before, pauses of 0.54 or 0.92 us, or of 1.22 us after each 8 gathers, don't end it: 1372.7, 1520.1 and 1440.3 us of "remote" before the row addition, for 1151.0 us.
- A gather that began right behind the start of a VectorE instruction of 1.22 us with two SBUF inputs lasted 1.97 us; under a reduction of the same length with one input one kept its 0.94 us.
- The granted clock follows TensorE's idle time: 0.95 in the good stretch, 0.56 in the bad one, where it stood idle for 18.39 and then 36.19 us, and 1.00 from 5000 to 6000 us in the kernels that gather nothing, or every second tile.
